# Fused transformer block, drain of the log attention: row numbers made in the step of their pages, GpSimd's sends begun a step sooner, one inverse deviation taken a step later

## What is computed

```python
x = x + linear_attention(layernorm(x), W_qkv, W_out)          # 16 heads of 8, rotary
x = x + ffn(layernorm(x), shared and routed weights)
x = x + log_attention(layernorm(x), w_qkv, w_ky, w_proj)      # 16 heads of 8, causal
x = x + ffn(layernorm(x), the same shared and routed weights)
```

```python
shared = silu(xt @ sg_w.T) * (xt @ su_w.T) @ sd_w.T
probs = sigmoid(xt @ router_w.T + routing_bias)
topk_p, topk_idx = top_k(probs, 2); topk_p /= topk_p.sum(-1)
routed = sum over the two chosen e of topk_p * (silu(xt @ wg[e].T) * (xt @ wu[e].T)) @ wd[e].T
```

## Time and profile before

| what | value |
|---|---|
| median of 3 runs | 1026.62 us (1026.45 to 1029.6) |
| time of the profiled execution | 1028.43 us |
| span of the profiled execution, first to last instruction | 1026.6 us |
| TensorE busy | 822.4 us, 80% |
| VectorE busy | 734.5 us, 72% |
| GpSimd busy | 589.0 us, 57% |
| ScalarE busy | 568.4 us, 55% |
| mean granted TensorE clock | 0.904 of full |

### The profile page before, as it was taken

One profiled execution on the slowest core, in us unless ns is written; L12 is line 12 of the kernel. 1 busy time (PEld: TensorE's weight loads), 2 busy tenths in 40 slices (PEclk: granted clock), 3 DMA queues, 4 the chain that ended last, 5 costly groups with the idle time before them and its releaser, 6 DMA issues. The chain is left out here.

```text
span 1026.6 us, 19542 instructions
## 1 busy us (share of the span) xinstructions
PE 822.4 (80%) x6459; PEld 546.7 (53%) x6459; DVE 734.5 (72%) x1506; ACT 568.4 (55%) x805; POOL 589.0 (57%) x815
## 2 busy tenths in 40 slices
PE   4887587899997777888888888979795678899890
PEld 2676466798985333333333333333352267898880
DVE  3888845455564658899999998999779645565574
ACT  1454142233345577989898989998763251233230
POOL 2343585881274566665644444455317877788783
PEclk9899678999997787999999999999877598999996
DMA  9990012123338477474837473732210121132443
GB/s 270 303 131 1 19 36 72 52 81 114 101 92 239 140 215 225 121 221 127 227 100 220 111 226 104 231 99 63 62 42 24 34 75 39 40 102 81 135 136 119
DMA packets 114402, 124.00 MB, mean 121 GB/s; under 512 B 13329, under 2 KB 76561, under 8 KB 114177
## 3 DMA queue, kind: packets, MB, share of 16 engines
q1 hardware_dynamic: 96512, 100.80, 35.8%
q0 software_dynamic: 8416, 17.29, 5.4%
q10 hardware_dynamic: 9376, 4.65, 1.6%
HBM read 59.97 MB, written 62.72 MB: 120 GB/s over the span
## 5 line engine op out<-in xcount | busy, mean ns | idle before, releaser
L2070 DVE TENSOR_SCALAR ring_b<-psum 128x1024 int32<-128x1024 int32 x160 | 194.2, 1217 | 25.1 <-PE psum L1765 23.9
L1930 ACT ACTIVATE ring_a<-psum 128x1024 f32<-128x1024 f32 x160 | 162.4, 1021 | 47.3 <-PE psum L1765 45.8
L1936 ACT ACTIVATE ring_b<-ring_b 128x1024 f32<-128x1024 f32 x160 | 168.7, 1055 | 34.5 <-DVE ring_b L2070 34.1
L2198 POOL TENSOR_SCALAR_AFFINE_SELECT ring_b<-ring_b 128x512 f32<-128x512 f32 (+1 forms) x112 | 80.3, 730 | 171.6 <-ACT ring_b L1936 171.3
L1765 PE MATMUL psum<-stacks 32*128 32x128 f32 (+3 forms) x1024 | 99.8, 389 | 59.6 <-DVE ring_b L2070 39.8
L1765 PEld LDWEIGHTS psum<-stacks 32*128 32x128 f32 x1024 | 57.6, 195 | 164.6 <-ACT ring_a L1930 75.7
L2062 DVE TENSOR_SCALAR ring_a<-ring_a 128x1024 f32<-128x1024 f32 x160 | 119.3, 751 | 11.7 <-ACT ring_a L1930 11.7
L949 ACT ACTIVATE ring_b<-psum 128x512 f32<-128x512 f32 x72 | 42.6, 592 | 116.5 <-PE psum L834 116.5
L1818 PE MATMUL psum<-ring_b,values 128*32 128x256 f32 (+3 forms) x1024 | 96.5, 488 | 8.2 <-POOL ring_b L2198 8.2
L1797 PE MATMUL psum<-ring_a,ones_s 128*32 128x256 f32 (+3 forms) x1024 | 93.0, 473 | 10.1 <-POOL ring_a L2198 9.2
L1448 DVE TENSOR_TENSOR ring_b<-psum,ring_b 128x512 f32<-128x512 f32 x72 | 49.2, 683 | 67.7 <-ACT ring_b L949 67.7
(11 more groups left out here) (220 smaller groups left out, 1480.5 us busy)
## 6 DMA issues: line engine op xcount, KB each, us to landing
stack_q<-parts SPq DMA_DIRECT2D x32, 256.0 KB
stack_ky<-parts SPq DMA_DIRECT2D x32, 256.0 KB
stacks<-stack_q SPq DMA_DIRECT2D x64, 128.0 KB, 3.4
stacks<-stack_ky SPq DMA_DIRECT2D x64, 128.0 KB, 3.9
stack_k<-parts SPq DMA_DIRECT2D x32, 256.0 KB
stacks<-stack_k SPq DMA_DIRECT2D x64, 128.0 KB, 3.0
stack_qr<-parts SPq DMA_DIRECT2D x32, 256.0 KB
stacks<-stack_qr SPq DMA_DIRECT2D x64, 128.0 KB, 2.6
```

Source lines behind the costliest of these rows:

```text
L1930: nc.scalar.activation(exps[:, n % RING, 2 * u:2 * u + 2, :], psum[:, first:first + 2, :], ACT.Exp, scale=SCALE).then_inc(self.exp, 1)
L1936: nc.scalar.activation(part, part, ACT.Ln, bias=1.0).then_inc(self.ln, 1)
L2070: nc.vector.tensor_scalar(ring[:, m % RING, HEADS_B[u][0]:HEADS_B[u][1] + 1, :].bitcast(I32), psum[:, first:first + 2, :].bitcast(I32), 0x ...
L2198: ins = nc.gpsimd.affine_select(out=part, in_=part, pattern=[[0, part.ap[1][1]], [1, 128]], compare_op=ALU.is_ge, fill=0.0, base=0, channe ...
```

## The change

Three places in two functions of `Experts`, and the index that goes with them in `pool`:

```diff
@@ lead_pool
-                if 10 <= k < 18:
-                    self.send(p, 0, 3 * (k - 10), 3 * (k - 9))
-                if k == 19:
+                if 9 <= k < 17:
+                    self.send(p, 0, 3 * (k - 9), 3 * (k - 8))
+                if k == 20:
                     self.pool_rstd(p, B)
-                if 18 <= k:
-                    self.send(p, 1, 3 * (k - 18), 3 * (k - 17))
+                if 17 <= k:
+                    self.send(p, 1, 3 * (k - 17), 3 * (k - 16))
@@ pool
-                    self.send(p, 1, 3 * (2 * DUS + 3 - 18))
+                    self.send(p, 1, 3 * (2 * DUS + 3 - 17))
@@ lead_vector
                 if k in (8, 13):
                     self.vector_gates(v, (8, 13).index(k))
                     self.vector_pages(v, (8, 13).index(k))
-                if k in (9, 14):
-                    self.vector_rows(v, (9, 14).index(k))
+                    self.vector_rows(v, (8, 13).index(k))
```

## The result

The kernel after takes 1033.71 us (median of 20 runs) beside 1026.81 us of the kernel before in as many runs on the same chip: a ratio of 1.0058, 95% interval 1.0033 to 1.0084. The kernel after is slower. The forecast was 1027.2 us, with a range up to 1030.8. Three more runs of the same kernel gave 1.0079, 1.0036 and 1.0055.

A forecast was written before the change was run, and what follows sets the result against it. GpSimd was taken as the bound, in the drain and the last scatters. Inverse deviation 2.9 us later (1.8 drain, 1.1 place), against a 2.4 us backlog, put the first scatter +0.6 us: 1026.62 to 1027.2 us, range 1024.2 to 1030.8.

The forecast's parts named there:

- Sends begun sooner: Chunk one's rows, moved to step 8, ready 2.27 us after VectorE's pages; GpSimd's first send at 772.1 instead of 775.86.
- the case of two inputs: GpSimd contends with VectorE instructions having two SBUF inputs, so rows are cheap where GpSimd idles; otherwise first send at 773.1.
- The drain: GpSimd's list from first send to last mask takes 43.3 us, so that mask is issued 1.8 us later; bounds 0.5 to 2.8.
- Its place in the list: Batch 8's inverse deviation, behind 12 sends instead of 9, starts 19.5 us after the last mask; 1.1 us of its 2.9 delay.
- The clock: Rival: TensorE's wait ahead of the down product grows to 3.4 us, its clock drops, quad 0 comes 3.2 us later; chance 0.22.
- The cover of 2.4 us: GpSimd's first scatter ran 2.4 us behind quad 0's data; its list gets free sooner, so that much of the delay is hidden.
- The last stage: From GpSimd's first scatter to the end of the kernel, taken as a fixed 130 us.
- The sum: First scatter at 897.15 instead of 896.60, so +0.6 us on the median, giving 1027.2 us.

The follow-up runs named there:

- e7: The kernel before with VectorE's part of the change alone, row numbers in steps 8 and 13; ratio 0.9975 to the kernel before.
- e3: The kernel before with one part of the change alone, batch 8's inverse deviation in step 20 instead of 19; ratio 1.0022 to the kernel before.
- e10: The changed kernel with 14 matmuls that nobody reads in TensorE's wait ahead of the down product; ratio 1.0022 to the kernel before.
- e9: The changed kernel again, unedited; ratio 1.0036 to the kernel before.
- e2: The changed kernel with batch 8's inverse deviation back in step 19, earlier sends and rows kept; ratio 0.9997 to the kernel before.
- e11: The changed kernel with batch 8's inverse deviation one step further, in step 21; ratio 1.0096 to the kernel before.
- e4: The changed kernel with two sends instead of three in steps 10, 13, 14, 15 and 19; ratio 0.9951 to the kernel before.
- e12: The changed kernel with the sends of e4 and one send fewer in each of steps 17 and 18; ratio 1.0027 to the kernel before.
- e16: The same kernel as e12, run again; ratio 0.9994 to the kernel before.
- e5: The changed kernel with 12 matmuls that nobody reads in TensorE's wait ahead of the down product; ratio 1.0011 to the kernel before.
- e8: The changed kernel with the inverse deviation back in step 19 and two pauses between variance and inverse deviation; ratio 0.9979 to the kernel before.
- e15: The same kernel as e4, run again; ratio 0.9971 to the kernel before.

## Why the prediction was wrong

**Sends begun sooner: right.** Forecast 2.27 us from the end of the pages to the rows; it was 773.15 less 771.04 = 2.11. The Trainium skill, GPSIMD Engine Reference, section 8 (Key points), on the interfaces that GpSimd and VectorE share, agrees in direction: with GpSimd idle beside them the rows were cheap, 2.11 against the 3.28 of the earlier trace rows. The largest single difference is in the last operation (0.18 us against 0.76), which reads one input, so the case of two inputs that the prediction named does not cover it. The move cost VectorE nothing that a run can measure (e7).

**The drain: its list right, its cost not settled.** From the first send to the last mask 43.3 us were forecast and 42.80 measured. What that costs against the kernel before hangs on how soon its first send would have come, and that differs between executions of one drain. Counted from the end of the pages, the last mask of the kernel after stands 1.12 us later than in the trace of before and 1.17 sooner than in that of e3; 1.8 later was forecast, with bounds of 0.5 and 2.8. Here too a distance of one trace was taken for a constant.

**Its place in the list: the first step that failed.** The prediction wrote that the inverse deviation starts 2.9 us later, "1.8 from the drain and 1.1 from its own place in the list". The 19.5 us from mask to deviation were right (19.43 to 19.49 in each run with these 12 sends). What it was measured against was wrong: 18.36 us of one trace, taken for a constant. That figure is the chain of the variance, which runs over TensorE at a clock that differs from execution to execution, and can be 16.1. The term is 1.1 us in some executions and 3.3 in others, and no lower bound of the old distance was asked for.

**The clock: put at nothing in the sum, and the rival that came true.** The sum has no term for it; as a rival it had a chance of 0.22. The prediction placed the deciding point between waits of 2.2 and 3.6 us and the new wait at 3.4; it was 3.98 in the trace, and 5.95 in the early case, and the clock fell in all four traces of this kernel. Its price was put at 3.2 us; the traces have 1.2 to 1.6 us with the late variance (62.88 to 62.97 against 61.40 to 61.65) and 3.8 to 4.1 with the early one (65.47). So its size too was that of neither case. The Trainium skill, TensorE: Matmul & The Clock Gate, Part 1, with throttled as the default that activity releases, is borne out by the row at 838.00 of the kernel after and the one of e10. So the +0.6 and the rival's +3.2 were one chain: the same later deviation brings both, and both grow with an early variance.

**The cover of 2.4 us: right, and too small.** As forecast GpSimd's list lost its backlog and stood free early (gap 10.57 us against 7 forecast), and the delay beyond the cover reached the first scatter. One detail cost 0.5 us: behind a wait the scatter started 0.75 us after the end of the copy (900.01 less 899.26), where I took the 0.28 of a scatter behind its pause. The last stage, taken as a fixed 130 us, was 128.6 to 131.5 in the 18 traces; between the two of before and after it gave back 1.0 of the 3.41 us.

**The sum.** Forecast +0.6 us; the times show +4.6 to +6.9. With the late variance the first scatter stands 0.77 us further behind the last mask (83.77 less 83.00). With the early variance the changed kernel has 86.25 (e9) where the old place in the list has 80.90 (e7), +5.4. Of the 18 traces 7 have the early variance; mixed in that share the two cases give about 2.6 us (7/18 of 5.4 and 11/18 of 0.77), and with -1.2 to +1.1 for the drain 1.4 to 3.7. What makes the rest is not settled: profiled executions may be early less often than timed ones, and the clock may cost more in places that I have not found. That step 20 is the cause rests on e2 and e11. That a part of the cost is the clock behind TensorE's wait rests on the traces and on the four runs with the wait filled, and their share is rough.

## What to carry to other kernels

When a small operation that another engine waits for is moved behind more work, compare its new place with the earliest moment at which its input can be ready, not with the moment in one trace: a distance that runs over TensorE changes with the granted clock. An idle gap ahead of such an operation is cheap if the list has slack later, and filling it with deferrable work is a loss when the gap was the shield of the chain that sets the end. Take deferrable work from ahead of the operations that others wait for (e4), but only as much as the list behind can take (e12 and e16, by their mean).

## What the runs showed of the hardware

- The same instructions from the last mask to batch 8's variance took 17.8 to 18.3 us or 15.6 to 16.0 us, with nothing between. From the eighth to the twelfth us behind the mask TensorE was granted 0.50 to 0.57 in the eleven late traces and 1.00 in the seven early ones.
- The length of a wait does not decide alone whether the clock falls behind it. In or behind waits of 3.17 us (e5) and more it fell in each of eight traces, and behind 3.07 (e8) not in the next 7 us; but in e16 it fell behind a wait of 2.33 us, where the down product took 2.02 us in the other traces with that wait (before, e2, e4, e7, e12, e15):

```profile
828.14 3.65 PE L798 MATMUL psum<-w_expert,ring_b 128*128 128x128 f32 x16 [2.33 <-issue]
```

```profile
828.00:830.00 2.00, 1.86 (x9) 1.89 (x10) 0.04 (x1) 2.00 (x6) 1.72 (x3) 0.56 0.40 123
```

- GpSimd starts an indirect transfer 0.75 us behind the end of the copy that it stood waiting for, in the traces in which it waited for that copy (0.75 or 0.76 in thirteen), and 0.28 us behind its own pause.
